# Queries by keys in two tiles of 64 contraction rows, with the score banks re-cut by pair of quads

## The reference

```
x = x + attention(group_norm(x))        # 32 groups of 8 channels
x = x + lif(linear(group_norm(x)))      # 256 -> 256
```

```
attn = softmax(q @ k.T + bias[head] + mask[window])     # 64 x 64
out  = attn @ v
```

## Time and profile before

| | |
|---|---|
| time, median of 3 runs (lowest to highest) | 584.67 us (583.52 to 585.52) |
| time of the profiled execution | 585.74 us |
| its span, first to last instruction | 584.0 us |
| matmuls, weight loads | 6120, 6120 |
| DVE, ACT, POOL busy share of the span | 81%, 74%, 55% |
| mean granted TensorE clock | 0.966 of 2.4 GHz |

### The profile page before, as it was taken

The page is one execution under the profiler, slowest core; times in us unless marked ns, Lnnn a source line. Parts: engine busy times, 40 slices in busy tenths (PEclk is TensorE's granted clock), DMA queues, the critical chain, the costliest instruction groups (busy, mean ns, idle before and its releaser), DMA issues.

```text
span 584.0 us, 16922 instructions
## 1 busy us (share of the span) xinstructions
PE 500.2 (86%) x6120; PEld 449.5 (77%) x6120; DVE 471.2 (81%) x995; ACT 433.9 (74%) x1045; POOL 321.4 (55%) x413
## 2 busy tenths in 40 slices
PE   0166699999999999999999999999999797689870
PEld 0165588888988889898889898898899686689760
DVE  9865577888888788878888888888777775979998
ACT  2274678887888888888878887888888667679840
POOL 8122564456555655654464556555555447777640
PEclk9988889999999999999999999999999999889995
DMA  7111011211121111111111111111111110122223
GB/s 197 55 36 38 1 39 42 44 40 40 41 54 38 36 36 36 36 36 36 40 36 40 40 41 36 36 20 20 21 19 20 20 19 2 69 78 91 91 109 143
DMA packets 52638, 27.32 MB, mean 47 GB/s; under 512 B 38770, under 2 KB 44148, under 8 KB 52596
## 3 DMA queue, kind: packets, MB, share of 16 engines
q1 hardware_dynamic: 51872, 26.76, 16.9%
q10 hardware_dynamic: 724, 0.01, 0.1%
HBM read 9.97 MB, written 8.39 MB: 31 GB/s over the span
## 4 chain that ended last, share of the span: by engine, by line
PE 27%; issue 27%; POOL 23%; DVE 17%; ACT 5%; POOLq 1%; DVEq 0%; ACTq 0%
POOL p_lo L406 11%; POOL xc L393 5%; PE score_ps L966 4%; DVE xc L844 3%; POOL xn_lo L366 3%; PE pv_ps L998 3%; DVE charged L836 2%; PE proj_ps L888 2%; PE proj_ps L889 2%; PE proj_ps L890 2%; PE score_ps L975 2%; PE max_ps L938 2%; PE max_ps L932 2%; DVE w_raw L710 1%; DVE membrane L841 1%
## 5 line engine op out<-in xcount | busy, mean ns | idle before, releaser
L406 POOL TENSOR_TENSOR p_lo<-probs,p_hi 128x512 f16<-128x512 f32 x128 | 146.4, 1165 | 173.7 <-ACT p_hi L566 173.7
L565 ACT ACTIVATE probs<-score_ps 128x512 f32<-128x512 f32 x128 | 77.0, 601 | 29.3 <-PE score_ps L975 28.5
L742 DVE TENSOR_TENSOR v_lo<-proj_ps,v_hi 64x128 f16<-64x128 f32 x256 | 74.1, 289 | 24.0 <-ACT v_hi L487 21.2
L888 PE MATMUL proj_ps<-xn_hi,w_hi 128*128 128x256 f32 x256 | 77.0, 301 | 11.2 <-POOL xn_lo L366 11.2
L749 DVE TENSOR_REDUCE neg_max<-max_ps 128x16 f16<-128x1024 f32 x64 | 78.4, 1225 | 4.6 <-PE max_ps L938 2.5
L452 ACT ACTIVATE xn<-xc,shift,rstd 128x256 f32 (+1 forms) x128 | 70.3, 605 | 14.4 <-DVE shift L231 7.6
L487 ACT ACTIVATE v_hi<-proj_ps 64x128 f16<-64x128 f32 x256 | 71.5, 279 | 10.6 <-PE proj_ps L900 7.6
L566 ACT ACTIVATE p_hi<-score_ps 128x512 f16<-128x512 f32 x128 | 77.4, 605 | 0.0
L889 PE MATMUL proj_ps<-xn_lo,w_hi 128*128 128x256 f32 x256 | 73.7, 288 | 0.0
L890 PE MATMUL proj_ps<-xn_hi,w_lo 128*128 128x256 f32 x256 | 73.5, 287 | 0.0
L966 PE MATMUL score_ps<-q_hi,k_hi 128*128 128x256 f16 x256 | 69.8, 273 | 0.0
(11 more groups left out here) (158 smaller groups left out, 1601.0 us busy)
## 6 DMA issues: line engine op xcount, KB each, us to landing
xc<-in_x_dram SPq DMA_DIRECT2D x32, 256.0 KB, 3.1
out_dram<-xc SPq DMA_DIRECT2D x32, 256.0 KB, 2.3
q_hi<-q_flat SPq DMA_DIRECT2D x128, 32.0 KB, 2.0
q_lo<-q_flat SPq DMA_DIRECT2D x128, 32.0 KB, 1.9
w_raw<-in_qkv_w_dram SPq DMA_DIRECT2D x1, 768.0 KB, 7.2
bias_raw<-in_bias_table_dram SPq DMA_DIRECT2D x16, 32.0 KB
w_raw<-in_lif_w_dram SPq DMA_DIRECT2D x1, 256.0 KB, 9.0
probs<-in_qkv_b_dram ACTq DMA_DIRECT2D x4, 0.5 KB
```

The lines of the kernel that those rows point to most:

```text
L406: pool.tensor_tensor(p_lo[p][:, quads, :, :].rearrange("p g w i -> p (g w i)"), probs[:, quads, :, :].rearrange("p g w i -> p (g w i)"), p ...
L565: act.activation(probs[:, quads, :, :].rearrange("p g w i -> p (g w i)"), score_ps[:, h, :], ACT.Exp)
L742: last = dve.tensor_tensor(v_lo[2 * slot + p][rows, :, w, :, e, 0:D], v_part(p, w, e), v_hi[2 * slot + p][rows, :, w, :, e, 0:D], ALU.subt ...
L888: pe.matmul(dst, w_hi[:, c, cols], high[:, tok], start=(c == 0 and bias is None), stop=False)
```

## The change

The scores of two quads need only 64 contraction rows: quads 0 and 1 lie on partitions 0 to 63, quads 2 and 3 on 64 to 127. The change calls these pairs of quads m = 0 and 1. Each matmul of L966 with 128 contraction rows and 256 columns becomes two, with 64 contraction rows and 128 columns each, one on partitions 0 to 63, one on 64 to 127, standing next to each other in the list and writing to different banks. For that the banks are re-cut: bank m holds both halves, of each the two quads of pair m. The same multiplications with non-zero operands are made.

- Matmuls of L966 in a pair: 12 of 128 rows x 256 columns before, 24 of 64 rows x 128 columns after. Weight loads: 12 and 24, of 128 columns each.
- Order in `scores`: both banks' waits for p_hi_done and both banks' bias matmuls come first, then the transpose of the maxima, then all 24 matmuls, then the wait for max_rows and the eight matmuls with pick_max.
- ACT and POOL work by bank m as before by bank h, with the same sizes. The loop over h in them is renamed. `weigh_values` picks its probabilities from the new places. The number of all other matmuls stays.

```
-                for h in range(HALVES):
-                    wait(pe, p_hi_done, n * 2 + (h - 1))
-                    for g in range(QUADS):
...
+                for m in range(2):
+                    wait(pe, p_hi_done, n * 2 + (m - 1))
+                    for h in range(HALVES):
+                        for q2 in range(2):
+                            at, g = (2 * h + q2) * 128, h * QUADS + 2 * m + q2
+                            if variant(k, 0) == variant(k, 1):
+                                pe.matmul(score_ps[:, m, at:at + 128], bias_k[:, variant(k, 0), g, :],
+                                          both_parts[:, :, :].rearrange("p w i -> p (w i)"),
+                                          start=(h == 0 and q2 == 0), stop=False)
+                                continue
+                            for w in range(2):
+                                pe.matmul(score_ps[:, m, at + w * WS:at + (w + 1) * WS], bias_k[:, variant(k, w), g, :],
+                                          both_parts[:, 0, :], start=(h == 0 and q2 == 0 and w == 0), stop=False)
+                turn_maxima(n)
                 for h in range(HALVES):
                     for w in range(2):
                         wx = 2 * p + w
-                        dst = score_ps[:, h, :].rearrange("p (g w i) -> p w g i", g=QUADS, w=2)[:, w, :, :]
                         at_q = (h * WCOLS + wx) * WS
-                        high = q_hi[slot][:, h, wx, :, :]
-                        for keys, queries in ((k_hi, high), (k_hi, q_lo[slot][:, :, at_q:at_q + WS]), (k_lo, high)):
-                            pe.matmul(dst, keys[slot][:, h, wx, :, :].rearrange("p e j -> p (e j)"), queries,
-                                      start=False, stop=False)
-                    if h == 0:
-                        turn_maxima(n)
+                        for keys, low_queries in ((k_hi, False), (k_hi, True), (k_lo, False)):
+                            for m in range(2):
+                                rows, quads = slice(64 * m, 64 * m + 64), slice(2 * m, 2 * m + 2)
+                                queries = q_lo[slot][rows, quads, at_q:at_q + WS] if low_queries else q_hi[slot][rows, h, wx, quads, :]
+                                dst = score_ps[:, m, :].rearrange("p (h q w i) -> p h w q i", h=2, q=2, w=2)[:, h, w, :, :]
+                                pe.matmul(dst, keys[slot][rows, h, wx, :, :].rearrange("p e j -> p (e j)"), queries,
+                                          start=False, stop=False)
                 pe.wait_ge(max_rows_done, n + 1)
-                for h in range(HALVES):
+                for m in range(2):
                     for w in range(2):
-                        for mid in range(2):
-                            dst = score_ps[:, h, :].rearrange("p (m q w i) -> p m w q i", m=2, q=2, w=2)[:, mid, w, :, :]
-                            last = pe.matmul(dst, pick_max[:, 4 * w + 2 * h + mid, :],
+                        for h in range(HALVES):
+                            dst = score_ps[:, m, :].rearrange("p (h q w i) -> p h w q i", h=2, q=2, w=2)[:, h, w, :, :]
+                            last = pe.matmul(dst, pick_max[:, 4 * w + 2 * h + m, :],
                                              max_rows[p][:, :].rearrange("p (q i) -> p q i", q=2),
-                                             start=False, stop=(w == 1 and mid == 1))
+                                             start=False, stop=(w == 1 and h == 1))
                     last.then_inc(score_ps_done, 1)
```

More of the change, by code:

```diff
@@ L402, in pair @@
                 wait(pool, pv_ps_done, n - 1)
-                for h in range(HALVES):
-                    pool.wait_ge(p_hi_done, n * 2 + (h + 1))
-                    quads = slice(h * QUADS, (h + 1) * QUADS)
+                for m in range(2):
+                    pool.wait_ge(p_hi_done, n * 2 + (m + 1))
+                    quads = slice(m * QUADS, (m + 1) * QUADS)
                     pool.tensor_tensor(p_lo[p][:, quads, :, :].rearrange("p g w i -> p (g w i)"),
@@ L560, in pair @@
                 wait(act, pv_ps_done, n - 1)
-                for h in range(HALVES):
[L562 to L566, removed]
+                for m in range(2):
+                    wait(act, p_lo_done, n * 2 + (m - 1))
+                    act.wait_ge(score_ps_done, n * 2 + (m + 1))
+                    quads = slice(m * QUADS, (m + 1) * QUADS)
+                    act.activation(probs[:, quads, :, :].rearrange("p g w i -> p (g w i)"), score_ps[:, m, :], ACT.Exp)
+                    act.activation(p_hi[p][:, quads, :, :].rearrange("p g w i -> p (g w i)"), score_ps[:, m, :], ACT.Exp)\
                        .then_inc(p_hi_done, 1)
@@ L997, in weigh_values @@
                         for at, (pp, vv) in enumerate(((p_hi, v_hi), (p_hi, v_lo), (p_lo, v_hi))):
-                            last = pe.matmul(cols[:, :, g, :], pp[p][:, h * QUADS + g, :, :].rearrange("p w i -> p (w i)"),
+                            last = pe.matmul(cols[:, :, g, :], pp[p][:, g // 2 * QUADS + 2 * h + g % 2, :, :].rearrange("p w i -> p (w i)"),
                                              vv[k][:, h, :, g, :, :].rearrange("p w e d -> p w (e d)"),
```

## The result

| | before | after |
|---|---|---|
| time, median (lowest to highest) | 583.81 us (581.61 to 586.17, 13 runs) | 587.58 us (585.40 to 590.84, 13 runs) |
| time of the profiled execution | 585.74 us | 589.22 us |
| its span | 584.0 us | 587.5 us |
| mean granted TensorE clock | 0.966 | 0.946 |
| instruction blocks loaded for TensorE | 25 | 64 |

The changed kernel takes 1.0067 of the time before, with a 95% interval of 1.0048 to 1.0086. It is 3.8 us slower where I had forecast 17 us faster, and lies outside the range.

What follows compares the result with a forecast made beforehand. TensorE was taken to bound the kernel, with max_rows capping the gain: 50 pairs x 0.37 = 18.5, less 1 for the tie, 17.5 us off 584.67 gives 567 us; 8-in-10 range 561 to 581.

Steps and rivals of the forecast that it cites:

- What bounds the kernel: Attention loop: TensorE sets the pace, busy 103.44 of 105.4 us, with DVE and ACT close at 84%.
- What the matmuls cost: Score matmuls L966: twelve at 1.31 us a pair become 24 at 0.031, 0.74 us, if tiles run side by side.
- Rival 2: Score matmuls: the two tiles take turns, 24 x 0.056 + 0.09 = 1.43 us against 1.31; slower, 592 us; chance 0.14.
- What changing the tiling costs: Edges where the array changes shape on TensorE: three a pair instead of two, one more at 0.09 us.
- The cap by max_rows: Before pick_max: ACT's max_rows limits the gain to 0.38 us at p = 0 and 0.37 at p = 1; 0.37 taken.
- The pairs without gain: 14 pairs held by other waits gain nothing, 50 left; third pair's transpose to pick_max 1.07 us against 1.05.
- TensorE alone: TensorE's own gain in a pair, before other engines' waits: 1.31 - 0.74 - 0.09 = 0.48 us.
- Do other things bind earlier?: Check of other waits: most stay hidden; project_k against attn_cm an exact tie, 0.04 us on half the pairs, 1 us.
- The chances: Odds for the whole kernel's time: faster 0.80, same 0.05, slower 0.15; the forecast itself 0.53.

Runs made afterwards that it cites:

- full_out: Changed kernel with all 128 contraction rows in each of the 24 matmuls and TensorE's loop written out; 586.30 us, 1.0038 of before.
- before_out: Kernel before, with TensorE's loop over samples 1 to 5 written out five times; 584.84 us, 1.0004 of before.
- vlo_cut: tiles_out without three of the four v_lo subtractions of a pair's second window; 566.99 us, 0.9691 of before.
- values_merged: tiles_out with v_hi and v_lo of a row's two pairs in one buffer, made by half as many, twice as long instructions; 559.25 us, 0.9563 of before.
- tiles_out: Changed kernel with TensorE's loop over samples 1 to 5 written out five times, other engines still looping; 571.88 us, 0.9786 of before.
- before_merged: Kernel before, looped and without tiles, with only the merged v_hi and v_lo instructions; 580.36 us, 0.9917 of before.
- full_loop: Changed kernel, looped, with its 24 matmuls at all 128 contraction rows instead of 64; 606.17 us, 1.0366 of before.

## Why the prediction was wrong

**What bounds the kernel**: right. TensorE set the pace, and shedding 0.54 us of it per pair brings up to 0.5 once its list and its partners allow.

**What the matmuls cost**: right, 0.68 us measured for 0.74. Two tiles take the time of one; the weight loads keep up at one per 0.028 us. Rival 2, with its 1.34 us, would have needed the 0.11 per two of full_out. That rival forecast a slower kernel, but not by this mechanism, and its sign is no credit.

**What changing the tiling costs**: right, 0.09 us, one edge more. The draining that the Trainium skill's "TensorEngine Tiling (Array Packing)" names isn't seen to cost more at the tiles than at the transpose.

**The cap by max_rows**: right in place and size. From p = 0 to p = 1 the intervals fell by 0.35 (forecast 0.38), 50 pairs wait, and moving max_rows ahead lowered them by 0.18 more. A row of two pairs was to lose 0.74 us; it lost 0.42 (13.19 to 12.77), for the reason below.

**The pairs without gain**: right in sum. The two intervals around the third pair went from 14.70 to 14.35, which is what one of the two pairs was to gain. The working counts an edge twice: the 0.15 behind the transpose has its 0.09 in it, so the 1.07 should be 0.98, 0.07 less than the 1.05 of before. It changed nothing in the sum, since the next projection waits for GpSimd's chain.

**The step that failed** is "TensorE alone". I counted what the 24 matmuls cost in the stream and put the supply of the longer list at nothing, without a reason. The change adds 12 matmuls and 12 weight loads in each of the 8 pairs of the loop body, 192 entries, and with 1666 in place of 1474 the body no longer stays with TensorE. Every jump back costs 4 us: 2.3 to 2.6 of standing still, in two of the four 0.6 or 1.2 more, and at three of them 1.0 to 1.6 more for projections at half the clock. Four jumps are 16 us; measured between looped and written out, 15.7. None of the rivals had it. The row that would have raised the question was on the page of before: 25 blocks of instructions, fewer than eight samples of 8 pairs written out would need (before_out loads 48), so the body was being kept, and something must bound what can be kept. Where that bound lies no row of before shows.

The Trainium skill, "Runtime: NRT & Kernel Launch", Instruction fetch mechanics, says that the engines' instructions come in blocks of 16 KiB and that a taken branch to a target outside the current window of two pages waits for the transfer. The runs agree with the size, 0.41 MB in 25 blocks, and with the stalls, but not with a window of two: bodies of 1474 to 1618 entries, some six blocks by an estimate with the page's 256 instructions to a block, jump back without a wait. It puts TensorE's room at 2048 instructions, by which the body of 1666 would have stayed; here it did not, so the measurement decides. It gives no duration; the 4 us are from the intervals above.

**The step that was mis-sized** is "Do other things bind earlier?". I had checked the projection of keys against attn_cm and found a tie, priced 0.04 us on half the pairs. Ahead of it the projection of queries had 0.04 us of cover behind v_lo, and I had not looked at that one. v_lo let the interval from p = 1 to p = 0 gain 0.07 instead of 0.37; attn_cm was then done 0.31 before the projection of keys (205.02, 205.33) and held nothing. Without v_lo the tie comes into play, at 0.14 and not 0.04, and the interval gains 0.14 more (vlo_cut); without both, and without the cap at p = 1, it gains 0.47 more (values_merged). By the forecast a sample would lose 7 x 0.37 less 0.15 for the ties, 2.4 us; without jumps it loses 54.5 - 52.7 = 1.8. The 0.6 that are missing are the 0.3 in each of the intervals 2 and 8, and over 6 to 7 samples they make some 4 of the 5.6 us between the forecast gain of 17.5 and the 11.9 of tiles_out.

**The chances**: 0.80 for faster and 0.15 for slower came from a list of rivals that were all about time on an engine. None was about the program's size.

What stays open: where between 1618 and 1666 entries the limit lies; what the 4 us of before_merged outside the loop are; and at which jumps the clock falls, which makes little difference in the kernel after (at most 0.25 us a jump) and some 2.5 us at the one jump of full_loop where it happened.

## What to carry to other kernels

Where a change multiplies the instructions inside a hardware loop, count the loop's body per engine, weight loads included, and compare the blocks of the instruction queue with what the body would need: a body of 1618 entries on TensorE was kept here and one of 1666 was not, and writing the loop out cost nothing. When an engine sheds work, check every wait of its list for its distance to what it waits for, and not only the one you have in mind: a cover of 0.04 us kept 0.3 of 0.37 us in two pairs of eight, and behind it stood the next wait, worth 0.14. And when a change is made for one engine's sake, the waits that it uncovers are worth a second edit: with TensorE's list written out, the tiles alone brought 12 us, with the merged values and the earlier maxima 29.

## What the runs showed of the hardware that I had not expected

- TensorE keeps a loop body of 1618 list entries (28 blocks in the whole run) and reloads one of 1666 after each jump (64 blocks), at 4.0 us per jump. With full-height matmuls it is 3.8 to 4.3 where the clock stayed at 1.00.
- Behind the wait of 2.31 us for the list TensorE's matmuls went at the lower clock, 1.2 GHz, from some 220.1 to 223.5 us: a float32 projection every 0.21 us instead of 0.12. Behind waits of 2.59 and 1.23 us at 275.92 and 278.97 they went at the full clock.
- A matmul of 64 rows by 128 columns with its own weight load can be issued every 0.028 us when the two row halves alternate; with full height it is 0.056.
- A change of the array's shape costs 0.09 us, the same for the transpose and for the tiles.
